# Score tiles of the maxima taken two heads at a time, in two halves of TensorE's rows

## What is computed

```python
xn = group_norm(x, g1, beta1)                       # 32 groups
q, k, v = split(einsum('oc,bchw->bohw', w_qkv, xn)) # 8 heads x 16 channels x 1024 positions
attn = einsum('bhdi,bhdj->bhij', q, k) * temp
attn = softmax(attn, axis=-1)                       # 1024 x 1024 for each head
out = einsum('bhdj,bhij->bhdi', v, attn)
x = x + einsum('oc,bchw->bohw', w_out, out) + b_out
x = x + mlp(group_norm(x, g2, beta2))
```

## Time and profile before

| what | value |
|---|---|
| three runs | 2105.62, 2107.11 (median), 2115.0 us |
| span of the profiled execution | 2109.6 us |
| instructions | 23070 |
| mean granted TensorE clock | 0.918 |

### The profile page before, as it was taken

The page is one execution under the profiler, slowest core; times in us unless marked ns, Lnnn a source line. Parts: engine busy times, 40 slices in busy tenths (PEclk is TensorE's granted clock), DMA queues, the critical chain, the costliest instruction groups (busy, mean ns, idle before and its releaser), DMA issues.

```text
span 2109.6 us, 23070 instructions
## 1 busy us (share of the span) xinstructions
PE 1830.4 (87%) x7380; PEld 944.4 (45%) x7380; DVE 1072.8 (51%) x1941; ACT 870.3 (41%) x1530; POOL 184.6 (9%) x189
## 2 busy tenths in 40 slices
PE   6678679988998889988998889988998889888886
PEld 3344344455545454445444445454544344444332
DVE  4241584557445654547355663556554655554701
ACT  1022114444444444444344443444444444454562
POOL 5003002100110001100120001100020001100000
PEclk9789789999999999989899898999999989999997
DMA  2000102010101010010100101010100110011000
GB/s 45 10 10 1 30 1 40 1 31 1 31 21 31 1 21 12 21 31 1 32 21 14 18 2 30 21 31 1 31 10 13 19 24 7 11 31 31 10 1 10
DMA packets 19567, 37.35 MB, mean 18 GB/s; under 512 B 8742, under 2 KB 10990, under 8 KB 19440
## 3 DMA queue, kind: packets, MB, share of 16 engines
q1 hardware_dynamic: 18352, 35.21, 8.7%
q0 software_dynamic: 1088, 0.53, 0.3%
HBM read 5.98 MB, written 4.20 MB: 5 GB/s over the span
## 4 chain that ended last, share of the span: by engine, by line
PE 50%; issue 32%; DVE 11%; ACT 3%; SPq 2%; DMA 1%; POOL 1%; ACTq 0%; DVEq 0%; POOLq 0%
PE ps L970 50%; DVE mx L944 6%; DVE mx L880 1%; SPq L401 1%; ACT p L663 1%; DMA kp<-k3l 0%; POOL mv L478 0%; DVE mv L769 0%; ACT vT L597 0%; SPq L415 0%; DVE x L828 0%; DVE x L827 0%; DVE sg L842 0%; DVE pg L808 0%; ACT hn L584 0%
## 5 line engine op out<-in xcount | busy, mean ns | idle before, releaser
L944 DVE TENSOR_REDUCE mx<-ps 128x1 f32<-128x512 f32 x1024 | 674.4, 685 | 567.6 <-PE ps L970 565.2
L663 ACT ACTIVATE p<-ps 128x512 f32<-128x512 f32 x1024 | 592.5, 598 | 767.2 <-PE ps L970 754.0
L970 PE MATMUL ps<-kp,qp 112*128 112x512 f32 x1024 | 470.7, 478 | 99.4 <-DVE mx L944 81.8
L970 PE MATMUL ps<-qp,kp 128*128 128x512 f32 x1024 | 492.7, 500 | 54.4 <-ACT p L663 35.3
L970 PEld LDWEIGHTS ps<-kp,qp 112*128 112x128 f32 x1024 | 197.9, 195 | 307.9 <-DVE mx L944 228.4
L970 PEld LDWEIGHTS ps<-qp,kp 128*128 128x128 f32 x1024 | 200.0, 201 | 246.7 <-ACT p L663 142.3
L970 PE MATMUL ps<-p,vt 128*32 128x512 f32 x2048 | 282.9, 627 | 0.0
L500 POOL TENSOR_TENSOR acc<-acc,p 128x512 f32<-128x512 f32 x96 | 122.7, 1278 | 332.0 <-ACT p L613 332.0
L970 PE MATMUL ps<-p,vT 128*128 128x512 f32 x256 | 151.1, 675 | 0.0
L613 ACT ACTIVATE p<-ps 128x512 f32<-128x512 f32 x128 | 76.5, 598 | 131.0 <-PE ps L970 131.0
L478 POOL TENSOR_TENSOR mv<-mv,neg_half 128x1 f32<-128x1 f32 x24 | 13.2, 551 | 1079.1 <-DVE mv L779 1079.1
(11 more groups left out here) (200 smaller groups left out, 1701.1 us busy)
## 6 DMA issues: line engine op xcount, KB each, us to landing
qp<-q3h SPq DMA_DIRECT2D x128, 64.0 KB, 2.4
kp<-k3h SPq DMA_DIRECT2D x128, 64.0 KB, 2.4
xin<-in_x SPq DMA_DIRECT2D x8, 512.0 KB, 3.7
qp<-q3l SPq DMA_DIRECT2D x64, 64.0 KB, 2.4
kp<-k3l SPq DMA_DIRECT2D x64, 64.0 KB, 2.4
out<-p SPq DMA_DIRECT2D x8, 512.0 KB, 2.8
qp<-nm3T SPq DMA_DIRECT2D x64, 4.0 KB
p<-padded_taps POOLq DMA_DIRECT2D x32, 16.0 KB, 2.1
```

The lines of the kernel that those rows point to most:

```text
L663: a.activation(p3[:, s % 2, i, :], ps[:, SB + p % 2, :], ACT.Exp).then_inc(sem("p3_ready"), 1)
L944: v.tensor_reduce(mx3[:, i, c, h:h + 1], ps[:, MB + n % 2, :], AX.X, ALU.max).then_inc(sem("mx3_ready"), 1)
L970: return nc.tensor.matmul(o, l, r, start=start, stop=stop)
```

## The change

The maxima's tiles of two heads go in a pair: two matmuls one behind the other, of rows 0 to 47 and of rows 64 to 111, into the two banks `MB` and `MB + 1`, and one reduction over both banks. `kp` gets two heads in one tile like `qp`, set to 1.0 once instead of to zero, so that row 48 of each half stays ones; the maxima go to row 48 of each half. The exponentials' product uses 49 rows, at 0 or at 64 by the head. The pairs come in even laps alone, and a pair waits for the reduction of the pair before it, not of the tile before the last. The zeroing of `qp` by GpSimd and the 8 DMAs of ones go.

```diff
-ROWS = 64 + PACK
+SPAN = 64
+PAIRS = GH // 2 * NC * NH
-MAXIMA_TILES = ("00000020220320222011110001212211121100011212222220231001011110000000",
-                "00000002200222202200110212131120220112022031020220311200002020000000")
+MAXIMA_PAIRS = ("0000111211112111121111211112111000",
+                "0000111211112111121111211112111000")
 def maxima_at(g, p):
-    tiles = [int(n) for n in MAXIMA_TILES[g]]
-    first = sum(tiles[:p])
-    tiles = range(first, first + tiles[p])
-    return tiles[:1], tiles[1:]
+    if p % 2:
+        return (), ()
+    counts = [int(n) for n in MAXIMA_PAIRS[g]]
+    first = sum(counts[:p // 2])
+    pairs = range(first, first + counts[p // 2])
+    return pairs[:1], pairs[1:]
...
-        kp = sb("kp", [128, HEADS, N], F32R)
+        kp = sb("kp", [128, HEADS // 2, N], F32R)
...
-                sp.wait_ge(sem("ones_ready"), 1)
-                sp.wait_ge(sem("packs_zeroed"), 2)
-                for hd in range(HEADS):
-                    r = 126 + hd % 2
-                    sp.dma_start(raw(kp[r:r + 1, hd, :]).rearrange("p (a b) -> p a b", b=128),
-                                 raw(ones_r[0:NC, :])).then_inc(sem("k_ones_in"), 16)
+                sp.wait_ge(sem("k_ones"), 1)
...
-                for dst, parts in ((qp[:, hd // 2, :], (q3h, q3l, q3h)), (kp[:, hd, :], (k3h, k3h, k3l))):
+                for dst, parts in ((qp[:, hd // 2, :], (q3h, q3l, q3h)), (kp[:, hd // 2, :], (k3h, k3h, k3l))):
...
-                                r = 126 + hd % 2
+                                r = SPAN * (hd % 2) + PACK
...
-                g.memset(raw(qp[:]), 0.0).then_inc(sem("packs_zeroed"), 1)
...
-                v.memset(raw(kp[:]), 0.0).then_inc(sem("packs_zeroed"), 1)
+                v.memset(raw(kp[:]), 1.0).then_inc(sem("k_ones"), 1)
...
-                u = mg * TILES + n
-                wait(dve, sem("s3max_ps"), mb, NG * TILES, u + 1)
-                i, c, h = n // (NC * NH), n // NH % NC, n % NH
-                v.tensor_reduce(mx3[:, i, c, h:h + 1], ps[:, MB + n % 2, :], AX.X, ALU.max).then_inc(sem("mx3_ready"), 1)
+                u = mg * PAIRS + n
+                wait(dve, sem("s3max_ps"), mb, NG * PAIRS, u + 1)
+                i, c, h = 2 * (n // (NC * NH)), n // NH % NC, n % NH
+                v.tensor_reduce(mx3[:, i:i + 2, c, h], ps[:, MB:MB + 2, :], AX.X, ALU.max).then_inc(sem("mx3_ready"), 1)
...
-                wait(pe, sem("mx3_ready"), mb, NG * TILES, mg * TILES + n - 1)
-                mm(ps[:, MB + n % 2, :], part(qp[0:ROWS, hd // 2, :], c), half(kp[0:ROWS, hd, :], hh)).then_inc(sem("s3max_ps"), 1)
+                wait(pe, sem("mx3_ready"), mb, NG * PAIRS, mg * PAIRS + n)
+                for e in range(2):
+                    rows = slice(SPAN * e, SPAN * e + PACK)
+                    last = mm(ps[:, MB + e, :], part(qp[rows, m, :], c), half(kp[rows, m, :], hh))
+                last.then_inc(sem("s3max_ps"), 1)
...
-                            hd, u = GH * g + i, g * TILES + p
+                            m, u = (GH * g + i) // 2, g * TILES + p
+                            rows = slice(SPAN * (i % 2), SPAN * (i % 2) + PACK + 1)
                             wait(pe, sem("p3_ready"), bt, NG * TILES, u - 1)
-                            mm(ps[:, SB + p % 2, :], part(kp[:, hd, :], j), half(qp[:, hd // 2, :], h)).then_inc(sem("s3_ps"), 1)
+                            mm(ps[:, SB + p % 2, :], part(kp[rows, m, :], j), half(qp[rows, m, :], h)).then_inc(sem("s3_ps"), 1)
```

More of the change, by code:

```diff
@@ L394, in pack @@
                 hd = GH * g + i
-                r, c = 64 * (hd % 2), HD * hd
+                r, c = SPAN * (hd % 2), HD * hd
                 if i == 0:
                     wait(sp, sem("vt3_ready"), bt, NG, g + 1)
-                for dst, parts in ((qp[:, hd // 2, :], (q3h, q3l, q3h)), (kp[:, hd, :], (k3h, k3h, k3l))):
+                for dst, parts in ((qp[:, hd // 2, :], (q3h, q3l, q3h)), (kp[:, hd // 2, :], (k3h, k3h, k3l))):
                     for n, part3 in enumerate(parts):
@@ L954, in passes @@
                         if maxima and p == M_END:
-                            wait(dve, sem("mx3_ready"), mb, NG * TILES, (mg + 1) * TILES)
+                            wait(dve, sem("mx3_ready"), mb, NG * PAIRS, (mg + 1) * PAIRS)
                             v.tensor_reduce(nm3[:], mx3[:].rearrange("p i c h -> p (i c) h"), AX.X, ALU.max,
@@ L1240, in scores_in_rows @@
             def scores_in_rows(n, mb, mg):
-                hd, c, hh = GH * mg + n // (NC * NH), n // NH % NC, n % NH
-                if n % (2 * NC * NH) == 0:
-                    wait(pe, sem(f"packed{hd % GH // 2}"), mb, 16 * 12 * NG, 16 * 12 * (mg + 1))
+                m, c, hh = GH // 2 * mg + n // (NC * NH), n // NH % NC, n % NH
+                if n % (NC * NH) == 0:
+                    wait(pe, sem(f"packed{n // (NC * NH)}"), mb, 16 * 12 * NG, 16 * 12 * (mg + 1))
                 if n == 0:
                     wait(pe, sem("nm3T_ready"), mb, NG, mg)
-                wait(pe, sem("mx3_ready"), mb, NG * TILES, mg * TILES + n - 1)
-                mm(ps[:, MB + n % 2, :], part(qp[0:ROWS, hd // 2, :], c), half(kp[0:ROWS, hd, :], hh)).then_inc(sem("s3max_ps"), 1)
+                wait(pe, sem("mx3_ready"), mb, NG * PAIRS, mg * PAIRS + n)
[3 more added lines that the diff above has]
+                last.then_inc(sem("s3max_ps"), 1)
             def passes(bt, sides):
@@ L1256, in passes @@
                     pe.wait_ge(sem("wo_in"), 16 * HEADS)
-                    pe.wait_ge(sem("k_ones_in"), 16 * HEADS)
-                    pe.wait_ge(sem("packs_zeroed"), 2)
+                    pe.wait_ge(sem("k_ones"), 1)
                 heads = bt.exists()
```

## The result

| | before | after |
|---|---|---|
| median of the runs | 2106.42 us (4 runs, 2105.62 to 2115.0) | 2590.85 us (4 runs, 2559.27 to 2607.69) |
| median as used below | 2106.42 us | 2567.67 us (2 runs, 2559.27 and 2576.07) |
| ratio after / before, 95% interval | | 1.2168 [1.2111, 1.2225] |
| span of the profiled execution | 2109.6 us | 2606.0 us |
| mean granted TensorE clock in it | 0.918 | 0.693 |

The change costs 22%, where 2% was forecast (2149 us, range 2035 to 2270). The direction is right, the time far outside. The time at half clock is worked out as in the prediction: the clock is 1.0 or 0.5, so a mean of 0.693 means that it stood at half for 61% of the span.

A forecast was written before the change was run, and what follows sets the result against it. PE's own queue was taken to set the pace, with DVE's reduction a local second bound. 2109.6 - 98 - 150 + 80 + 19 + 120 = 2081 us, + 70 for the clock, less 2.5, gave about 2149 us; range 2035 to 2270.

The forecast's parts named there:

- What bounds the kernel: Whole window: PE's own queue sets the pace (50% of the chain); locally, DVE's reduction of the maxima holds PE.
- Part 1: Maxima on PE: 512 pairs run both row halves at once, less late second loads; -98 us, bounds 0 and -118.
- Rival D: Maxima pairs: rows don't overlap, a pair costs 0.46 us, sum 2179 us at an unchanged clock; chance 0.09.
- Part 2: PE's waits for DVE's reduction: most go, -150 us; second pairs in a lap +80, lost double buffer +19.
- The second pairs: Five laps of a half hold two pairs; 80 second pairs each wait about 1.0 us: +80 us, bounds +30 and +130.
- Part 3: PE's changes between half and full height: some 800 new borders at 0.15 us, +120 us, bounds +80 and +160.
- Part 5: TensorE's granted clock: half-clock time grows by some 200 us at 0.35 each, +70 us, bounds 0 and +200.
- Sum at an unchanged clock: Whole kernel, all terms but the clock's: 2109.6 - 98 - 150 + 80 + 19 + 120 = 2081 us.
- Rival B: Whole kernel faster: clock stays and the sides' steps cover the reduction; 2022 to 2050 us, nearest 2055; chance 0.31.

The follow-up runs named there:

- e3: Kernel before with its schedule, double buffer and single tiles, but both score products at half height (48 and 49 rows): 2581.99 us, ratio 1.2218.
- e1: Changed kernel with both score products back at the old full heights, keeping the order in pairs, single buffer and two-bank reduction: 2239.19 us, ratio 1.0604.
- e9: Full-height pair kernel of e1 with its pairs spread, at most one in a lap, odd laps too: 2235.86 us, ratio 1.058.
- e6: Kernel before with a 48-row, 2-column product added ahead of each exponential product, making two borders: 2400.7 us, ratio 1.1338.
- e7: Kernel before with a 2-column product over all rows added ahead of each exponential product, no new border: 2174.82 us, ratio 1.0283.
- e8: Kernel before with both score products over rows 0 to 64 in place of 128 and 112 rows: 2290.48 us, ratio 1.0857.
- e2: Changed kernel with the exponentials' products back at 128 rows, the maxima still in half-height pairs: 2345.24 us, ratio 1.1087.
- e12: Changed kernel with the third block's one-row product of the maxima padded with zeros to 128 rows: 2387.15 us, ratio 1.1346.
- e10: Kernel before with the third block's one-row product of the maxima padded with zeros to 128 rows: 2052.01 us, ratio 0.9691.
- e4: Changed kernel with one more product over 128 rows, overwritten, ahead of each exponential product: 2951.1 us, ratio 1.3967.
- e11: Changed kernel with its pairs spread one to a lap over laps 8 to 60: 2464.17 us, ratio 1.1639.

## Why the prediction was wrong in size, by its steps

**What bounds the kernel: right.** PE's queue sets the pace, and a slower PE showed one for one: the chain gives it 68% after for 50%, and every other engine only waits longer.

**Part 1, the pair (-98): the mechanism right.** Pair start to reduction is 0.54 us, one tile's was 0.53. Rival D is out. The number -98 is near for reasons that the prediction did not have. More products start together than the 512 that it counted: 678, since exponential products also fall in with tiles of the other half, even without pairs (e3). Against that, half-height products that follow each other otherwise stand mostly 0.34 us apart in place of 0.23, which no term of the sum has.

**Part 2, waits for the reduction (-150, +80, +19): wrong.** The sign, not only the size. 1.22 us for the reduction over two banks was right (1225 ns). But the waits were to fall from 228 to some 100 us, and are 209.7, with PE's own idle time at 127.0, up from 81.8. The argument was that a pair in every second lap leaves 3.56 us for a cycle of 1.9; it took the laps as even in time. In e1, which has this part alone, the kernel lost 123 us in place of gaining 51. Of these an estimated 114 x 0.36 = 41 us are clock and about 80 are waits; PE's idle time behind the reduction grew by 77. So the step was wrong by some 130 us. The second pairs, the +80, are not it: e9 has none and gained 3 us. Two banks in alternation let PE run one tile ahead, and the pair takes that away; that this is the reason is what is left over, and not shown by a run of its own.

**Part 3, the borders (+120): right, within some 30 us.** Up to 0.20 at one place (0.43 in place of 0.23), 0.14 for each at the one-row product and 0.13 in e6 and e7, for the 0.15 taken; 759 new ones for the 800 taken; so 91 to 106 us for 120 at 0.12 to 0.14 each. At half clock a border costs more, 0.22 at the one-row product, which the prediction did not have.

**Part 5, the clock (+70): the mechanism and the price right, the size wrong, and this is the step that failed.** The sentence was: "I expect the half-clock time to grow by some 200 us", with 450 as the bound and a clock of 0.87 or less. It grew by 1155 us, to 1501, at clocks of 0.704 and 0.711 (in the profiled execution by 1254, to 1600, at 0.693). The price for each was to be 0.35. It is 0.36 in e8, where nothing else changes. Over the whole change it is 456 / 1155 = 0.40 (456 us is the growth of the span) and in e3 471 / 1130 = 0.42, but these two hold borders and overlap as well. The guess that matmuls which leave most of the array idle hold the clock up less was called a guess from few spells; e8 shows it alone, and so does the step from e2 to the changed kernel; e12 shows it backwards. What went wrong was to treat it as a surcharge on spells that were already at half. The half-height products are 2048 of 7380, in every lap of every window, so the clock fell in stretches that had been at full, as the line of the page shows in nearly every slice. In the sum the term was the last and the smallest, at 70 us, though it was the only one with no row for its size. At the prediction's own price 1155 us would have been +404, and the forecast 2483 against 2567.67. So this one step is 334 of the 419 us that the forecast is short of that time. It also carries the direction: without it the forecast was 2081 us, faster than before.

**Sum at an unchanged clock (2081).** Taking 1155 us at e8's 0.36 from the mean span of 2565.9 leaves an estimated 2150. So the other terms together were some 70 us too low. Part 2 alone was 130 too low, so some 60 us must lie the other way, in the other terms or in a price that is lower in places: in the steps of the next paragraph it is 0.34 and 0.31.

How the 2567.67 - 2106.42 = 461 us come about, one part added to the other by medians: schedule and single buffer 2239.19 - 2116.1 = 123 (e1), the maxima at half height 2345.24 - 2239.19 = 106 (e2), the exponentials at 49 rows and what goes with them 2567.67 - 2345.24 = 222. That is 451, the rest being the 10 us by which before differs between the chips. The two steps that change rows raise the time at half clock by 316 and 725 us, 0.34 and 0.31 us for each. In e2 the 106 us are the sum of an overlap that saves and of borders and clock that cost. Between e2 and the changed kernel the pairs stay and the borders get fewer (1847 and 1660), so these 222 us come from the rows, nearly all through the clock: 725 us at 0.36 would be 261.

**Rival B** (faster, if the half-clock time grows by less than 80 us) set the right condition, and the condition failed: the half-clock time grew by 14 times as much.

**Open:** what share of e10's fall in time at half clock is the missing borders and what share the rows of zeros; what share the pauses at borders have in the fall of the clock from e1 to e2, where new borders and fewer rows come together; how e4's 1168 further borders and its full-height work balance; and why spreading the pairs helps at half height (e11) and not at full height (e9).

## What to carry to other kernels

Where PE is the bound, look at what a change does to the rows that its matmuls use before counting the instructions saved: here half-height products put 1130 to 1155 us more at half clock, each cost 0.3 to 0.4 us, and no overlap paid for it. Padding a product with few rows with zeros up to 128 cost PE nothing in time here, took away its borders and went with a higher clock; 128 one-row products padded so made this kernel 3.1% faster, and the version to keep is e10, at 2052.01 us. And two tiles joined in one wait lost the run-ahead of two alternating banks: at full height that schedule cost 123 us (e1). Whether two pairs of banks would give it back, no run here shows.

## What the runs showed of the hardware

The granted clock follows the rows in use and not PE's busy share alone: PE is busy 87% of the span before and after, at 0.918 and 0.693, and with the same instructions in the same order the clock is 0.824 for 65 rows against 0.918 for 128 and 112 (e8). Effects on the clock don't add up: the same padding took away 42 us at half clock in one kernel and 331 in another. A change between full and half height costs 0.13 us, here for 48 rows behind 112 and ahead of 128 (e6); by the Trainium skill's "TensorEngine Tiling (Array Packing)", section "Key Properties", that is the drain at a change of mode, and the traces agree with 0.43 for 0.23. Half-height products in different halves start within 0.01 us of each other, 678 times in the changed kernel and 385 times in e3; otherwise they are mostly 0.34 us apart at full clock, where full-height ones can follow at 0.23.
